# Six kinds of VectorE instruction cut into parts of 4 columns or 8 features

## The reference, cut to what matters

```
x = x + rel_conv(relu(layernorm(x)), src, dst, types)     # 16 relations, sum over edges
x = x + sage3(relu(layernorm(x)), src, dst)               # three mean aggregations
x = x + bi_interaction(relu(layernorm(x)), src, dst)
x = x + gat2(relu(layernorm(x)), src, dst)                # two attentions

def gatv2(x, src, dst, ...):
    s = leaky_relu(xl[src] + xr[dst], 0.2)
    e = einsum('ehc,hc->eh', s, att)
    alpha = softmax of e over the edges of one dst
    return segment_sum(xl[src] * alpha, dst) + bias
```

## Time and profile before

| | us |
|---|---|
| median of 3 runs | 6364.63 |
| lowest and highest | 6355.12, 6367.59 |
| the profiled execution | 6354.62 |
| its span | 6352.9 |

### The profile page before, as it was taken

The page is one execution under the profiler, slowest core; times in us unless marked ns, Lnnn a source line. Parts: engine busy times, 40 slices in busy tenths (PEclk is TensorE's granted clock), DMA queues, the critical chain, the costliest instruction groups (busy, mean ns, idle before and its releaser), DMA issues. The chain is left out here.

```text
span 6352.9 us, 77087 instructions
## 1 busy us (share of the span) xinstructions
PE 3817.5 (60%) x19708; PEld 2604.5 (41%) x19708; DVE 4159.4 (65%) x13369; ACT 2294.0 (36%) x6083; POOL 4278.3 (67%) x4026
## 2 busy tenths in 40 slices
PE   3777788888288878866763444566466557760000
PEld 1444455555155545544543444455355423330000
DVE  6999799999544444434443665666599767765443
ACT  0000477777311111113334555222233279980000
POOL 5777777777677767767775775777300188884777
PEclk9999899999555555555555555788666689985555
DMA  1111344333233333334542454233244445552221
GB/s 40 50 47 47 120 158 158 115 112 100 70 101 106 89 94 97 97 94 128 152 139 81 147 151 132 92 93 94 70 162 173 154 116 141 150 126 78 88 87 63
DMA packets 413613, 684.98 MB, mean 108 GB/s; under 512 B 283685, under 2 KB 290444, under 8 KB 407978
## 3 DMA queue, kind: packets, MB, share of 16 engines
q1 hardware_dynamic: 282410, 542.14, 24.0%
q0 software_dynamic: 130944, 140.05, 11.1%
HBM read 310.94 MB, written 373.78 MB: 108 GB/s over the span
## 5 line engine op out<-in xcount | busy, mean ns | idle before, releaser
L711 POOL DMA_INDIRECT G<-states,srcq x1568 | 1608.5, 1026 | 488.5 <-issue 476.5
L1807 PE MATMUL PS<-ident,HH 128*128 128x128 f32 x2357 | 543.2, 380 | 936.5 <-ACT AT L2076 279.9
L1346 DVE SCALAR_TENSOR_TENSOR R<-R,same,G 128x64 f32<-128x64 f32 x1568 | 447.7, 286 | 829.0 <-DMA G<-states,srcq 645.3
L1807 PEld LDWEIGHTS PS<-ident,HH 128*128 128x128 f32 x2357 | 383.2, 197 | 1044.9 <-issue 481.9
L2076 ACT COPY AT<-PS 128x512 f32<-128x512 f32 (+1 forms) x494 | 283.7, 580 | 1047.6 <-PE PS L1822 719.4
L1822 PEld LDWEIGHTS PS<-WD,AT 128*128 128x128 f32 x2358 | 498.1, 312 | 178.9 <-issue 178.5
L824 POOL DMA_INDIRECT out_nodes<-O,dstq x392 | 432.2, 1103 | 187.5 <-issue 123.3
L1822 PE MATMUL PS<-WD,AT 128*128 128x64 f32 x2358 | 552.6, 412 | 0.0
L711 POOL DMA_INDIRECT EE<-node_info,srcq x392 | 412.5, 1052 | 134.4 <-issue 134.4
L711 POOL DMA_INDIRECT G<-states,srci x392 | 417.3, 1064 | 119.4 <-issue 118.8
L711 POOL DMA_INDIRECT PG<-in_x,dsti x392 | 406.6, 1037 | 119.4 <-issue 118.5
(11 more groups left out here) (413 smaller groups left out, 10053.8 us busy)
## 6 DMA issues: line engine op xcount, KB each, us to landing
states<-O SPq DMA_DIRECT2D x70, 896.0 KB, 3.8
HH<-states SPq DMA_DIRECT2D x56, 896.0 KB
total<-R SPq DMA_DIRECT2D x56, 896.0 KB, 3.7
XB<-resid SPq DMA_DIRECT2D x42, 896.0 KB, 6.1
states<-HH SPq DMA_DIRECT2D x28, 896.0 KB, 5.0
G<-states,srcq POOLq DMA_INDIRECT x1568, 2.5
resid<-XB SPq DMA_DIRECT2D x28, 896.0 KB, 6.8
xl_of_src<-O SPq DMA_DIRECT2D x14, 1792.0 KB, 6.9
```

Of the source, the lines that this page charges most:

```text
L711: return pool.indirect_dma_start(to, None, table_, bass.IndirectOffsetOnAxis(ap=idx, axis=0), bounds_check=bound, oob_is_err=False).then_i ...
L1346: row = dve.scalar_tensor_tensor(out=R[:, b, j * D:(j + 1) * D], in0=row_before, scalar=same[:, bass.ds(i * C + j, 1)], in1=G[:, b, j * D: ...
L1807: last = pe.transpose(PS[:, 4 + k, q * P:(q + 1) * P], HH[:, b, (g * G4 + q) * D2:(g * G4 + q + 1) * D2], ident[:])
```

## The change

`by_parts` does a two-input instruction in parts of `size` columns of its middle axis, with no wait between the parts. It is put in place of one long instruction at the residual sums of layers 2 and 3, the tail mask of the first attention, the node sums, the mask, the sum and the product of the second attention, the weighting and the three result steps. The second attention's scan is cut into 8 scans of 8 features each, and its leaky part into 7 of 4 columns. The mask there is cut along features, 8 at a time. The sums are the same, element by element; a scan of 8 features starts at zero, as a feature's flags do.

```diff
+        FEATS_AT_ONCE = 8
...
+            def by_parts(out_, in0, in1, op, size=G4):
+
+                n = out_.shape[1]
+                for at in range(0, n, size):
+                    some = slice(at, min(at + size, n))
+                    last = tt(out_[:, some], in0[:, some], in1[:, some], op)
+                return last
...
-                step(tt(XB[:, b, :], XB[:, b, :], O[:, b, 0:CD], ALU.add))
+                step(by_parts(cut(XB[:, b, :]), cut(XB[:, b, :]), cut(O[:, b, 0:CD]), ALU.add))
...
-                step(tt(cut(XB[:, b, :]), cut(XB[:, b, :]), over(tail[:, at], D), ALU.mult))
+                step(by_parts(cut(XB[:, b, :]), cut(XB[:, b, :]), over(tail[:, at], D), ALU.mult))
...
-                tt(RN[k % 3], RN[k % 3], XN[k % 7], ALU.add).then_inc(s_nadd, 1)
+                by_parts(cut(RN[k % 3]), cut(RN[k % 3]), cut(XN[k % 7]), ALU.add).then_inc(s_nadd, 1)
...
-                step(tt(turned, XB[:, b, :].rearrange("p (t f) -> p f t", f=D), tail[:, at].unsqueeze(1).broadcast_to([P, D, C]), ALU.mult))
+                step(by_parts(turned, XB[:, b, :].rearrange("p (t f) -> p f t", f=D), tail[:, at].unsqueeze(1).broadcast_to([P, D, C]), ALU.mult, FEATS_AT_ONCE))
...
-                dve.tensor_tensor_scan(out=one[:, ::-1], data0=flags[:, ::-1], data1=XC[:, ::-1], initial=0.0,
-                                       op0=ALU.mult, op1=ALU.add).then_inc(s_scan2, 1)
+                for f in range(0, CD, FEATS_AT_ONCE * C):
+                    some = slice(f, f + FEATS_AT_ONCE * C)
+                    last = dve.tensor_tensor_scan(out=one[:, some][:, ::-1], data0=flags[:, some][:, ::-1], data1=XC[:, some][:, ::-1], initial=0.0,
+                                                  op0=ALU.mult, op1=ALU.add)
+                last.then_inc(s_scan2, 1)
...
-                step(tt(cut(two), cut(NEAR[i % 4]), one.rearrange("p (f t) -> p t f", t=C), ALU.add))
-                step(dve.scalar_tensor_tensor(out=two, in0=two, scalar=0.2, in1=two, op0=ALU.mult, op1=ALU.max))
+                step(by_parts(cut(two), cut(NEAR[i % 4]), one.rearrange("p (f t) -> p t f", t=C), ALU.add))
+                for g in range(GROUPS):
+                    some = two[:, g * G4 * D:(g + 1) * G4 * D]
+                    last = dve.scalar_tensor_tensor(out=some, in0=some, scalar=0.2, in1=some, op0=ALU.mult, op1=ALU.max)
+                step(last)
...
-                step(tt(cut(two), cut(two), attb2[:].unsqueeze(1).broadcast_to([P, C, D]), ALU.mult))
+                step(by_parts(cut(two), cut(two), attb2[:].unsqueeze(1).broadcast_to([P, C, D]), ALU.mult))
...
-                step(tt(cut(o), cut(r), inverse, ALU.mult))
-                step(tt(cut(o), cut(o), bias2b[:].unsqueeze(1).broadcast_to([P, n, D]), ALU.add))
-                return tt(o, o, xb, ALU.add)
+                step(by_parts(cut(o), cut(r), inverse, ALU.mult))
+                step(by_parts(cut(o), cut(o), bias2b[:].unsqueeze(1).broadcast_to([P, n, D]), ALU.add))
+                return by_parts(cut(o), cut(o), cut(xb), ALU.add)
...
-                step(tt(cut(G[:, b, :]), cut(G[:, b, :]), over(Eb[:, 0, at], D), ALU.mult))
+                step(by_parts(cut(G[:, b, :]), cut(G[:, b, :]), over(Eb[:, 0, at], D), ALU.mult))
```

## The result

The changed kernel took 6290.31 us (median of 4 runs, 6285.17 to 6292.84), the kernel before on the same chip 6366.11 us (4 runs, 6355.12 to 6373.02): 0.9881 of the time, with an interval of 0.9864 to 0.9899. That is 76 us faster where 126 us were forecast; the time lies 0.3 us above the end of the range. The profiled execution has a span of 6288.3 us against 6352.9 us.

What follows compares the result with a forecast made beforehand. POOL's row transfers, held behind long two-input VectorE instructions, were taken to bound these stages. Savings of 26 + 14 + 36 + 50 = 126 us from 6354.6 gave 6229, plus 10 for the median: 6239 us, range 6200 to 6290.

Steps and rivals of the forecast that it cites:

- the hold and its price: POOL transfers wait out a two-input VectorE instruction and enter at the next joint; seven parts cost VectorE 0.48 us more.
- layer 2: Residual sum (L1309) in seven parts: 26 us less for layers 2 and 3 together, 13 us each.
- the first attention: Tail mask (L1469) in parts: 14 x 1.0 = 14 us less; the mask's own 0.48 us hidden.
- the last sums: L1651, L1652, L1653 and L1659 in parts: 38 us of POOL's stretch less 1.9 us of VectorE, 36 us less.
- Rival D: Everywhere: joints without a wait don't let POOL in, so a train holds it 2.50 us; slower, 6458 us; chance 0.05.
- rival E: A gather that gets in keeps VectorE out for its remaining 0.87 us, so trains stretch; about 6411 us; chance 0.04.
- POOL waits for nobody there, so these stages last as long as its instructions: Layers, both attentions, last sums: POOL's idle time is nearly all "issue", about 0.30 us per transfer, 392 transfers per stage.
- the second attention: ScalarE takes over as bound: 57 us from waits and tail, less 7 us given back, 50 us less; ends 20 and 57.
- tail of 20 us: End of second attention, after ScalarE's last copy: VectorE needs about 6 us instead of 26, with the last gather in hand.
- with rows that come earlier the other eight, 35.2 us, go: Second attention: eight of ScalarE's nine waits for VectorE at L2254 vanish, because VectorE no longer waits for gathered rows.
- rival B: Second attention: VectorE's longer slots or late node rows keep ScalarE waiting; only the tail's 20 us come, 6269 us; chance 0.14.
- ScalarE near 100% and L2254's waits gone: Profile signs, second attention: ScalarE's share near 100% in the middle; the forecast is wrong if L2254's waits stay.

Runs made afterwards that it cites:

- the earlier scaling: Changed kernel with ScalarE's scaling of the next chunk in layers 0 to 3 done in the first three groups, ahead of its root: 6283.43 us, 0.9864 of before.
- nine buffers: Changed kernel with nine instead of seven buffers for node rows in the second attention: 6269.84 us, 0.9844 of the kernel before.
- SP's orders: Two runs, changed kernel, second attention: SP's store one slot and load three slots later, 6297.35 us; only the store later, 6269.55 us.
- three clears: Changed kernel with POOL also clearing an unread tile three times in each chunk of the second attention: 6273.08 us, 0.9842 of before.
- both limits moved: Changed kernel with nine node-row buffers in the second attention and ScalarE's scaling in layers 0 to 3 in the first three groups: 6248.26 us, 0.9806 of before.
- ten clears: Changed kernel with POOL also clearing an unread tile ten times in each chunk of the second attention: 6328.08 us, 0.9944 of before.
- nine-buffer control: Kernel before with nine instead of seven buffers for node rows in the second attention: 6369.37 us, ratio 1.0.

## Why the prediction was right and where it failed

**Right: the hold and its price.** That a transfer is held to the next joint, and that a joint without a wait lets it in, carried layer 2 (-12.0 for -13), the first attention (-12.0 for -14) and the last sums (-35.8 for -36). Parts of 14 columns, which gave back 15 us of the last sums, show that the length of a part sets what is left. The stretch that is left behind the parts of L1143 in the changed kernel is about 33 us, second attention included: 123 transfers that end 0.87 us after a part, each 0.27 us longer than 0.995; the parts of the scan and of the leaky part leave some 9 us more. At the 14 masks of the first attention it is 2.4 us, 0.17 for each train, where the forecast had 0.2. Rival D falls with the means of POOL, rival E with the parts' 420 ns. The Trainium skill ("SBUF — State Buffer", section on its two separate sides) has the lock held by whichever starts first, for its whole instruction; the runs show that for VectorE's side alone, since parts that start while POOL issues take no longer than the others.

**Wrong: "POOL waits for nobody there, so these stages last as long as its instructions".** In layer 3 a second limit lay as close: POOL needed 28 x (1.049 + 0.305) = 37.9 us for a chunk, and the loop from VectorE's sum over statistics, root and scaling back to VectorE's L1358 took 38.0 to 38.2 us for a chunk. In the changed kernel, where POOL needs 36.9 us, the loop still takes 38.1 to 38.4, and with parts of 14 columns, whose sum is shorter than that of 4, 37.8 to 38.0; the stage there is 3.5 us shorter, 576.5 us. An engine that shows only "issue" ahead of its instructions bounds a stage, but what it would gain is limited by the next bound, which the idle time of POOL cannot show. The row was in the profile: 98.4 us of waits for ScalarE in layer 3, none of them in layer 2, whose program does not have this wait. 13 us of the forecast failed here, and the run with the earlier scaling gave 14.4 back. These 13 us and the 31 us of the second attention, below, are 44 of the 50 us by which the forecast was too large.

**Wrong: the second attention, by 31 us.** The forecast's tail of 20 us was 13.8: from ScalarE's last copy to VectorE's last sum it took 26.45 us before and takes 12.65 now (ScalarE, then VectorE):

```profile
5684.07 0.58 ACT L2260 COPY O<-PS 125x512 f32<-125x512 f32 x1 [0.38 <-PE PS L1943]
...
5695.28 2.02 DVE L1654 TENSOR_REDUCE EE<-HH 128x28 f32<-128x1792 f32 x1
```

I had counted the sum, the product and the last sum there, and left out the leaky part and a node sum (2.44 and 1.43 us); the sum, with one input turned, takes 3.84 us in its parts. The larger error is the step "with rows that come earlier the other eight, 35.2 us, go", with 7 us given back for node rows that "don't arrive faster". ScalarE's waits fell from 68.0 to 61.9 us over the stage; 6.1 + 13.8 are the stage's 19.1 us within 1 us. The node rows did not merely keep their time, they came more slowly: in the middle of the stage a load took 14.4 us from issue to landing before (median of 42) and 19.0 us after (of 32). With gathers at full pace the queue of POOL took 40.4% of the DMA engines instead of 21.8%, and loads that had hidden behind waits for gathers came late, in place of them. This is rival B, with its price of 20 us, to which I had given 0.14.

ScalarE's own work in the stage is nearly the same before and after, 563.57 and 565.34 us, so the stage can be added up along it: what lies beside its waits for VectorE is this work, the start and the tail. One account holds across the runs: the stage less ScalarE's waits (at its root and, with nine buffers, for a store) is 638.2 us in the changed kernel, 638.4 with nine buffers, 639.0 and 639.2 with SP's orders, 635.4 with 14 columns, 638.2 with three clears and 637.9 with both limits moved; it is 638.9 with layer 3's sum whole and 639.5 with the earlier scaling. Where POOL is the bound it is more, 651.2 before, 653.4 with the stage whole again and 656.8 with ten clears, before and with the stage whole by the longer tail. So what an edit in this stage is worth beside the tail is read at ScalarE's root.

**Wrong signs of the profile after.** ScalarE near 100% and L2254's waits gone were named as what would show the step right, and "L2254's waits stay" as what would show it wrong: they stayed. POOL waits for stores there, as was named, 8.8 us in all. The last sums' sign, that POOL does not wait for L1653, held: POOL waits for it once, ahead of the first chunk.

**The stage that changed by itself.** The stage behind the first attention took 522.2 us before and 534.9 after, with the same code. Thirty us near its end (the granted clock is the number ahead of the DMA share), before and after:

```profile
5012.00:5042.00 30.00, 20.70 (x108) 16.01 (x108) 13.01 (x18) 10.32 (x25) 0.00 (x0) 0.74 0.34 145
```

```profile
5002.00:5032.00 30.00, 26.06 (x91) 19.68 (x90) 8.15 (x14) 8.70 (x21) 0.00 (x0) 0.50 0.33 138
```

TensorE ran at the lower of its two levels (1.2 GHz) throughout this stretch after the change, and at the higher (2.4 GHz) for about half of it before. The nine-buffer control, which is the kernel before in this stage, took 532.9 us, with a granted clock of 0.50 in the same stretch; the kernel with the second attention whole, which is the changed one there, 523.2 us, with 0.76. So the difference goes with the clock and not with the edit, and belongs to single profiles.

## What to carry to other kernels

Short two-input instructions on VectorE give POOL's transfers back what they are held for, and in a stage that POOL bounds the gain can be summed beforehand from the hold and the length of a part. What of it reaches the end is set by the second limit of each stage, so look for waits that do not name the bounding engine, and compare them between stages with nearly the same code. Before an engine is made faster, ask which transfers its slowness had kept apart: the same rows, gathered earlier than anyone needs them, made loads late that the next engine did need.

## What was not expected of the hardware

Each packet of the gathers kept a DMA engine longer when POOL ran at full pace (share x 16 engines x 300 us, divided by the packets): 0.218 x 16 x 300 / 5704 = 0.18 us before, 0.404 x 4800 / 6735 = 0.29 us after, 0.301 x 4800 / 6355 = 0.23 us with three clears. So the same work took more of the engines' time the closer it came together. Why it does was not tried, and stays open.

The loads of node rows in the middle of the stage, from issue to landing, show both the pace and the order on SP's queue. Right behind SP's two transfers of 896 KB they took 17.2 us before, 23.9 after and 19.9 with three clears; elsewhere 14.0, 16.4 and 14.9 (medians). So faster gathers went with longer loads everywhere, and most of all behind the large transfers. How much of the stage's loss is due to either alone stays open; each of three edits (more lead, another order, a slower POOL) took most of it away.
